# Far keys of the second layer: all of them gathered, each gather held by TensorE's progress, no one-hot products

## The reference

```python
I = jnp.einsum('bths,h->bts', relu(einsum('bthd,bsd->bths', q_i, k_i)), idx_w)
I = jnp.where(local, inf, I); I = jnp.where(causal, -inf, I)   # local: the last 64 keys
_, idx = jax.lax.top_k(I, 96)
key_c = (c_kv @ W_uk)[bi, idx]; value = (c_kv @ W_uv)[bi, idx]; kr_sel = (x @ W_kr)[bi, idx]
scores = (einsum(q_c, key_c) + einsum(q_r, pope(kr_sel))) * scale
out = einsum(softmax(scores), value) @ W_out
```

## Time and profile before

| | us |
|---|---|
| median of 3 runs | 2414.38 (2406.73 to 2421.93) |
| the profiled execution | 2407.81 |
| its span | 2406.0 |
| POOL busy, 1103 instructions | 1696.6 |
| gathers L1682, 320 | 321.3, mean 1.004 |
| compares L1854, 277 | 81.8, mean 0.357 |

### The profile page before, as it was taken

One profiled execution on the slowest core, in us unless ns is written; L12 is line 12 of the kernel. 1 busy time (PEld: TensorE's weight loads), 2 busy tenths in 40 slices (PEclk: granted clock), 3 DMA queues, 4 the chain that ended last, 5 costly groups with the idle time before them and its releaser, 6 DMA issues. The chain is left out here.

```text
span 2406.0 us, 61609 instructions
## 1 busy us (share of the span) xinstructions
PE 2097.7 (87%) x24894; PEld 1364.8 (57%) x24894; DVE 1847.7 (77%) x3743; ACT 1681.7 (70%) x3414; POOL 1696.6 (71%) x1103
## 2 busy tenths in 40 slices
PE   5899999999999999999999898553787787777888
PEld 2466666666666666666666565221465565545565
DVE  7788888888888888888884798564878976667434
ACT  4898998989989889899898465553655553544363
POOL 4899999999999999999998364543433334655500
PEclk8999999999999999999999898676988997877688
DMA  4000000000000000000000001111111111111101
GB/s 144 1 2 2 2 2 2 2 2 2 2 2 2 2 2 2 2 2 2 2 2 2 21 25 52 27 20 20 35 40 37 27 41 25 30 34 28 32 17 36
DMA packets 57653, 44.07 MB, mean 18 GB/s; under 512 B 34896, under 2 KB 47776, under 8 KB 57120
## 3 DMA queue, kind: packets, MB, share of 16 engines
q1 hardware_dynamic: 45856, 28.38, 4.3%
q0 software_dynamic: 11520, 11.82, 2.5%
HBM read 34.35 MB, written 1.61 MB: 15 GB/s over the span
## 5 line engine op out<-in xcount | busy, mean ns | idle before, releaser
L380 POOL TENSOR_TENSOR probs_lo<-probs,probs_hi 128x1024 f16<-128x1024 f32 x512 | 1076.9, 2131 | 42.9 <-ACT probs L430 42.3
L494 DVE TENSOR_REDUCE part_max<-aux 128x1 f32<-128x512 f32 x1024 | 677.3, 686 | 91.5 <-PE aux L568 87.0
L429 ACT ACTIVATE probs_hi<-scores 128x512 f16<-128x512 f32 x1024 | 630.2, 615 | 134.5 <-PE scores L601 116.5
L430 ACT ACTIVATE probs<-scores 128x512 f32<-128x512 f32 x1024 | 636.6, 622 | 0.0
L1682 POOL DMA_INDIRECT far<-key_table,placeT x320 | 321.3, 1004 | 394.1 <-PE a_score L1995 275.8
L617 PE MATMUL acc<-v,probs_hi 128*128 128x65 f16 x4096 | 451.1, 193 | 2.3 <-POOL probs_lo L380 2.3
L619 PE MATMUL acc<-v,probs_hi 128*128 128x64 f16 x4096 | 452.2, 195 | 0.0
L621 PE MATMUL acc<-v,probs_lo 128*128 128x65 f16 x4096 | 450.6, 192 | 0.0
L617 PEld LDWEIGHTS acc<-v,probs_hi 128*128 128x128 f16 x4096 | 382.5, 96 | 82.7 <-POOL probs_lo L380 2.5
L619 PEld LDWEIGHTS acc<-v,probs_hi 128*128 128x128 f16 x4096 | 380.0, 97 | 75.5
L568 PE MATMUL aux<-k_a,q_a 128*128 128x512 f16 x1024 | 392.0, 383 | 5.2 <-DVE roped L480 2.1
(11 more groups left out here) (333 smaller groups left out, 4112.8 us busy)
## 6 DMA issues: line engine op xcount, KB each, us to landing
far<-key_table,placeT POOLq DMA_INDIRECT x360
qT<-qT SPq DMA_DIRECT2D x16, 256.0 KB
queries<-places SPq DMA_DIRECT2D x7, 512.0 KB
e_w<-in_e_w SPq DMA_DIRECT2D x48, 64.0 KB, 1.9
near_value<-key_table SPq DMA_DIRECT2D x128, 12.0 KB
x<-in_x SPq DMA_DIRECT2D x4, 256.0 KB, 3.6
cos<-in_cos SPq DMA_DIRECT2D x1, 1024.0 KB, 7.3
sin<-in_sin SPq DMA_DIRECT2D x1, 1024.0 KB, 9.3
```

Of the source, the lines that this page charges most:

```text
L380: pool.tensor_tensor(probs_lo[:, slot], probs[:, wide], probs_hi[:, slot], ALU.subtract).then_inc(low_ready, 1)
L429: act.activation(probs_hi[:, slot, i], bank, ACT.Exp, scale=float(DH0) ** -0.5)
L430: act.activation(probs[:, wide, i], bank, ACT.Exp, scale=float(DH0) ** -0.5).then_inc(probs_ready, 1)
L494: dve.tensor_reduce(part_max[g % 2][:, n % QT, n // QT:n // QT + 1], bank, AX.X, ALU.max).then_inc(aux_free, 1)
```

## The change

All 32 far keys of tiles 1 to 15 are gathered (496 gathers, 456 of them in `selected_attention`), and everything of the one-hot products goes: `hot`, `make_keys`, `spread_places`, the fp16 split of the rows, 34 turn units and their copies. What a gather waits for changes too. The first 40 each wait for a filled bank of `projections1` (`full`, from the 14th to the 47th of 50). Those of `selected_attention` each wait for a turn unit of TensorE (`turn_full`). `paced` spreads tile t's gathers evenly over the turn units in slots 8(t-2) to 8(t-1); tiles 1, 2 and 3 have the slots 0 to 4, 4 to 12 and 12 to 18. A tile has 13 turn units now, so 2 or 3 gathers are let go by one, 3 or 4 in the slots of tile 3.

```diff
@@ -1205,6 +1207,8 @@
                     if i == 0:
                         pool.wait_ge(place_ready, t + 1)
+                    n = FIRST_JOB + (i + (gathers(0) if t else 0)) * PACED_JOBS // FIRST_GATHERS
+                    pool.wait_ge(full, n)
                     pool.indirect_dma_start(far[t][:, i, :], None, keep["table"][0:FIRST_ROWS, :],
...
-PER = 4
-UNITS = {t: 4 if t < 10 else 1 for t in range(3, NT)}
...
-    work += [("make", made // NG, made % NG)] if made % NG < UNITS.get(made // NG, 0) else []
...
-    work += [("hot", t, (j - MADE_AT) % NG)] if (j - MADE_AT) % NG < UNITS.get(t, 0) else []
...
-    return [(t, i) for t in range(NT) for i in range(gathers(t) - made(t))]
+    return [(t, i) for t in range(NT) for i in range(gathers(t))]
...
+        def paced(t, i):
+
+            done = FIRST_GATHERS - gathers(0) if t == 1 else 0
+            first, last = {1: (0, 4), 2: (4, 12), 3: (12, 18)}.get(t, (NG * (t - 2), NG * (t - 1)))
+            turns = [sum(w[0] in TURNS for slot in range(A_SLOT + j) for w in selected_schedule(slot, ranking))
+                     for j in (first, last)]
+            return turns[0] + (turns[1] - turns[0]) * (i - done) // (gathers(t) - done) + 1
...
-                def spread_places(t):
...
-                    if t > 2:
-                        pool.wait_ge(score_full, NG * (t - 2) + NG * i // (gathers(t) - made(t)) + 1)
+                    pool.wait_ge(turn_full, paced(t, i))
                     pool.indirect_dma_start(far[m][:, i, :], None, keep["table"],
...
-                        dve.tensor_scalar(hot_tile(t, k, kt), placeB[:, k * CH:(k + 1) * CH], key_id[:, kt:kt + 1], None,
-                                          ALU.is_equal).then_inc(hot_ready, 1)
...
-                                ins = pe.matmul(b[:, i * KW:(i + 1) * KW], hot_tile(t, k, kt)[:, i * P:(i + 1) * P],
-                                                split[:, kt, part * KW:(part + 1) * KW], start=(kt + part + i == 0),
-                                                stop=(kt == t and part == 1), skip_group_check=True)
```

More of the change, by code:

```diff
@@ L1062 @@
 FIRST_ROWS = T // 2
+FIRST_JOB = 14
+PACED_JOBS = 34
 TOP_OPS = 3 * (FAR // 8)
@@ L1545, in landed @@
 def landed(t, half):
-    each = lambda s: 16 if not half else 16 - made(s) if s else 0
-    return 16 * sum(each(s) for s in range(t % RING, t + 1, RING))
+    return 256 * (t // RING + (0 if t % RING == 0 and half else 1))
 def keys_no(t, half):
@@ L1581, in selected_attention @@
         probsT = sb("a1_probsT", [P, 2, NG, P], F32)
[L1582 to L1586, removed]
         biggest = sb("biggest", [P, NG], F32)
@@ L1603, in selected_attention @@
         schedule = [w for slot in range(A_SLOT + (NT + 1) * NG) for w in selected_schedule(slot, ranking)]
-        TURNS = ("q", "far", "make", "p", "y")
+        TURNS = ("q", "far", "p", "y")
         order = [w for w in schedule if w[0] in TURNS]
@@ L1701, in empty_turn @@
                         ins = act.activation(farT[:, i % 2, :, :], src[:].rearrange("k (i l) -> k i l", i=4), ACT.Copy)
[L1702 to L1706, removed]
-                        ins = act.activation(far[t % RING][:, first:first + PER, :],
-                                             src[:, 0:PER * KW].rearrange("p (i k) -> p i k", i=PER), ACT.Copy)
                     elif kind == "p":
@@ L1729, in _ @@
                 for kind, t, i in schedule:
-                    if (kind, t, i) == SPLIT_AFTER:
-                        act.wait_ge(turn_full, turn_no["q", 1, 3])
-                        act.activation(split[:, :, 0:KW], rows[:, 0:SPLIT, :], ACT.Copy).then_inc(high_ready, 1)
                     if kind in TURNS and kind != "y":
@@ L1885, in _ @@
                         dve.wait_ge(far_in[m][i], landed(t, i))
-                        if i and t in UNITS:
-                            dve.wait_ge(turn_free, free_no["make", t, UNITS[t] - 1])
                         every = lambda ap: ap[:].unsqueeze(1).broadcast_to([P, 16, ROPE1])
@@ L1924, in _ @@
             def _(pe):
-                def make_keys(b, t, k):
-                    if k == 0:
-                        pe.wait_ge(split_ready, 1)
-                    for kt in range(t + 1):
-                        pe.wait_ge(hot_ready, hot_no[t, k, kt])
-                        for part in range(2):
-                            for i in range(PER):
-                                ins = pe.matmul(b[:, i * KW:(i + 1) * KW], hot_tile(t, k, kt)[:, i * P:(i + 1) * P],
-                                                split[:, kt, part * KW:(part + 1) * KW], start=(kt + part + i == 0),
-                                                stop=(kt == t and part == 1), skip_group_check=True)
-                        if kt < t:
-                            ins.then_inc(hot_used, 1)
-                    return ins
                 def fill_turn(kind, t, i):
@@ L1947, in fill_turn @@
                         pe.wait_ge(turn_free, free_no[before])
-                    if kind == "make":
-                        make_keys(b, t, i).then_inc(turn_full, 1)
-                        return
                     if kind == "q" and i == 0:
@@ L2325, in tables @@
     t["unit"] = bfloat16(np.eye(P))
-    t["key_id"] = (P * np.arange(SPLIT)[None, :] + np.arange(P)[:, None]).astype(f32)
     t["iota"] = np.tile(np.arange(E0, dtype=f32), (P, 1))
@@ L2394 @@
     dram["out"] = nc.dram_tensor("out_0", (T, D), F32, kind="ExternalOutput").ap()
-    dram["places"] = nc.dram_tensor("places", (len(MADE), P * max(made(t) for t in MADE)), F16, kind="Internal").ap()
     dram["key_table"] = nc.dram_tensor("key_table", (T, KW), F32, kind="Internal").ap()
```

34 lines of the change are left out of this document (removed).

## The result

The change made the kernel slower: 2464.28 us (median of 4 runs, 2461.21 to 2471.11) against 2418.15 of the kernel before beside it (4 runs, 2406.73 to 2423.94), ratio 1.0231 [1.0195, 1.0266]. Forecast were 2359 us and a range of 2302 to 2430. The profiled execution took 2461.21 us.

The account below looks back on a forecast made before the run. No engine was full; gather runs withheld PE's signals, and after the change the gather queue would set the pace at 1.42 us each. 2407.8 - 40.3 - 7.5 - 8 = 2352.0, plus 6.6 for the median: 2359 us, range 2302 to 2430.

Parts of the forecast that it names:

- the first sign: Tile 0: no wait of ACT or DVE over 10 us, and the tile under 45 us.
- The third: Sign in ACT's and DVE's waits on "remote": many of 1 to 3 us, none of 10.
- the stop: POOL's pause after each group of gathers: 1.03 us late, making at most 4.1 us a group, 1.67 a gather.
- terms 3 and 5: Tile 0's stall of 40 us goes, counted at 39; the first 40 gathers, spread over filled banks, bring -8 us.
- Term 1: Compares, products, copies and spreading go: 0.47 us for each of 277 compares, 130 us; bounds 82 and 165.
- Term 2: 136 gathers more cost 0.50 us each, 68 us; bounds nothing and 1.25 each, 170.
- Tile 14: Loses 16 compares and has no gathers: -7.5 us.
- The wait more for each gather: One more wait ahead of each gather on POOL costs nothing.
- Stops eat the gain: Rival: stops between gather groups make 1.54 us a gather, 2413 us, no change; chance 0.16, its end 1.58 giving 2431.
- TensorE falls to its lower clock: Rival: without products PE sits at 1.2 GHz, 52 us a tile, 1.62 a gather, 2453 us; chance 0.12.
- The hold doesn't hold: Rival: units signalled together release long gather runs, so tile 0's 39 us stall stays; 2398 us, chance 0.06.
- Undisturbed: Rival: spaced gathers disturb nobody and POOL's floor alone counts, 1.29 us a gather; 2299 us, chance 0.16.

Follow-up runs that it names:

- late sets: Follow-up sets in which the kernel before takes about 2402 to 2407 us and TensorE's results are taken late by other engines.
- the run of 32: 32 gathers without a gap in the changed kernel without holds from gather 41 on, where TensorE's results are taken late; 2655.4 us, 1.1033.
- prompt sets: Follow-up sets in which the kernel before takes about 2258 us and TensorE's results are taken at once.
- set 2: Kernel before 2401.62 us; changed kernel 1.0197, with score holds from tile 3 1.004; kernel before with two one-hot units for four 1.0011, plus new holds 0.9841.
- the earlier trace: Profiled execution of the kernel before, from which the prediction was made; 2407.8 us.
- set 3: Kernel before 2405.77 us; with new holds added 0.9804; changed kernel less its 136 added gathers 0.9523, with fill products 1.0298, with 64-row gathers 1.0269.
- set 5: Kernel before 2407.23 us; changed kernel again 2455.53 us, 1.02; changed kernel without holds from gather 41 on 2655.4 us, 1.1033.
- The filler: Changed kernel with six more products of 256 bf16 columns in each turn unit, to keep TensorE from idling; 2478.59 us, 1.0298.
- the first trace: Profiled execution of the changed kernel in the main measurement; 2461.21 us.
- the holds alone: Kernel before with every gather held as in the changed kernel, one-hot products kept; 2356.11 us, 0.9804 late; 2264.32 us, 1.0031 prompt.
- two units with the holds: Kernel before with two one-hot units in place of four in tiles 3 to 9, and the new holds; 2365.26 us, 0.9841.
- an unheld variant: Changed kernel without holds on turn units or scores from gather 41 on; 2263.17 us, 1.0022 prompt; 2655.4 us, 1.1033 late.
- set 1: Kernel before 2257.61 us; with new holds 1.0031; changed kernel with old holds 1.0005, less 136 gathers 0.9582, with landing waits every fourth gather 1.1027.

## Why the prediction was wrong

**The reading it started from** (a run withholds TensorE's signals) held, for late sets: 3.2 us in the timeline of tile 4, 20.7 us in the run of 32, 78 of 78 `ctx` units late, nothing in prompt sets. It is too sharp: some units pass inside a run, seven `y` units in set 2 after 0.04 us. And only PE's results were seen late. The end of ACT's softmax sums reached an idle DVE after 0.03 us in all 44 cases within runs of seven late traces. The rule that I weighed against it, that a DMA never contends with a compute engine (the Trainium skill, SBUF — State Buffer, Who interferes with whom), agrees with the prompt sets, 0.03 us in the middle of a run. In late sets results of TensorE reach others late while gathers run. No run shows that this is contention for memory, so these sets neither refute the rule nor are explained by it.

**Which engine sets the pace** was right: gathers, from tile 1 on, the tiles alike whatever their ranking. So was the first sign, tile 0 at 31.9 us. The third failed: no wait on "remote" was to reach 10 us, and ACT's for `ctx` reach 15.2.

**The step that failed is the stop.** I priced it at 1.03 us over the plain gap, from four gathers in tile 4, and thought that early in a run units slip through. It is 2.76 - 0.31 = 2.45 us, well over twice that, after 7 gathers and not 2.5 to 5: 1.30 + 2.45/7 = 1.65 by this sum, 1.64 measured. The first term was small too, 1.25 for a gather and its gap that take 1.30. The 0.22 us between 1.64 and my 1.42 are 0.22 x 456 = 100 us, nearly the whole miss: 2359 + 100 = 2459. In the earlier trace rows the score that POOL waited for ended 0.26 us after the run, before even the plain gap of 0.30 was over. In the changed kernel the unit that a gather waits for often isn't done: PE itself stood still for a result of ACT that waited for a signal of PE. A late signal can be paid at each crossing of the chain, and `y` with its 3.75 us stands behind two. What the hold is tied to matters then: on scores 1.7 us a stop and 48.7 us a tile, on units 2.8 and 51 to 52. Both lie over my 45. How the stop divides into late signals, PE's own work and the low clock no run shows.

**The terms.** In set 3 the holds are worth 0.0196 x 2406 = 47 us; terms 3 and 5 had 48. That the sizes agree is partly luck: against the earlier trace rows tile 0 fell by 39.5 us, but tile 1 grew by 18.0, and the first 40 gathers brought 14.1 us, not 8. Term 1: (0.9804 - 0.9523) x 2406 = 68 us, not 130, and under my lower bound of 82. I had priced a compare from tiles 2 to 7 and charged it in tiles 9 to 13 too, where the gathers already hid it: 0.36 x 140 is 50 of the 68. Term 2, from sets 5 and 3: (1.0200 - 0.9523) x 2406 = 163 us for 136 gathers, 1.20 each, not 0.50 and close to the ceiling of 1.25. Two tiles with 28 gathers and with 1 gave me 0.50, but tile 14, with its 1, still had products that ruled it; the difference of two tiles with different bounds is no price. The three parts, -47 - 68 + 163, give the +48 us of set 5 by their making; they show where it comes from. In a prompt set the gathers cost (1.0005 - 0.9582) x 2258 = 96 us, 0.70 each, with the old holds on one side and the new ones on the other.

**Tile 14** gained 2.1 us (34.8 to 32.7), not 7.5. **The wait more for each gather** did not cost nothing: 2.7 us a tile from tile 3 on (set 2), over holds on scores.

**The rivals.** "Stops eat the gain" named the right mechanism, and its end of 1.58 was still too low. "TensorE falls to its lower clock" gave 52 us a tile, 1.62 a gather and 2453 us, all three almost as measured, and its mechanism did not come about: by it PE's work fills a tile with 48.8 us, and PE was busy for 36.0 of 52.5 in tiles 3 to 7 and for 35.0 of 52.3 in 9 to 13. The filler points the same way (0.77 for 0.65, and no time came back), though its own work blurs it. A share of the lower clock isn't excluded: PE's 25.7 us of work a tile grew to 35 or 36, and the tiles with a slow `y` are the longer ones by 2.6 us. How much of the loss that makes is open. "The hold doesn't hold" was half right, groups of seven instead of two or three. "Undisturbed" was seen in the prompt sets alone, and there with the old holds or none. My range left out the slow side because I capped the stop at 1.67 a gather as an extreme, when it was the rule.

The gathers' mean fell from 1004 to 989 ns. The estimate of 0.06 us each for the compares gone (DVE's 2-port mode, the Trainium skill, SBUF — State Buffer, Who interferes with whom) would have been four times that; I had left it out, and rightly. In set 3 the mean of 320 gathers is 1008 ns with the compares beside them and 1010 without, so the compares had no part in it at all.

**Best kernel.** In late sets the holds alone, 0.9804, and two units with the holds, 0.9841, beat both kernels and can't be told apart. In prompt sets nothing that computes the whole result beat the kernel before. A hold that leaves `y` out of its count might avoid the longest stops; it wasn't tried.

## What to carry to other kernels

Price a wait by the longest chain that it can starve, not by the delay of one signal: count how often the work ahead of it crosses between engines. Price an operation in the stage where it goes; one that lies behind a queue already full is worth nothing, however dear it was elsewhere. And a rival that gives the measured time isn't shown by that; take away its cause and look.

## What the runs showed of the hardware

- The same kernel takes 2258 or 2405 us, on chip 9 both, by the set. Tiles 9 to 13 of the kernel with the holds alone take 170.8 or 237.8 us, and an unheld variant 2263 or 2655. The two kinds differ in how late TensorE's results reach others while POOL issues gathers: an idle ACT took a `ctx` unit 0.04 us after its end in every prompt trace, and 3.6 to 5.3 us after it in the median in the late ones where all keys are gathered and held by units. What decides between the two kinds is open; it isn't the chip alone. A verdict on such a change needs both kinds, and whoever schedules gathers should hold them: in the kernel with its products 0.3% lost in a prompt set, 2% won in a late one.
- POOL issues a gather of 128 rows of 256 bytes at best every 1.25 us, in unbroken runs 1.30 in the mean, in prompt sets and late ones alike (996 ns busy in set 1 and 989 in the first trace, and a gap of 0.30 us). One of 64 rows keeps it busy for 952 ns, not for half of 989.
- In late sets the records also miss semaphore events while gathers run: from the first gather to the last the first trace of the changed kernel has 436 of PE's 509, 425 of ACT's 653 and 476 of DVE's 788, and ahead of the gathers all of them. That may be why so many waits there are named "remote" or "issue".
